# A cross-attention and mixture-of-experts kernel: the first tile's splits on other engines, two orders changed at the seam, and the last slot's weights in other buffers

## The chip, the cores and the metric

The kernel runs on one core of a Trainium2 chip. A core has five engines with their own instruction streams: PE (TensorE, matmuls), ACT (ScalarE), DVE (VectorE), POOL (GpSimd) and SP (SyncE, which here only issues DMAs). They wait for each other through semaphores. The metric is the device time in microseconds of one execution, from launch to end; lower is better.

## What is computed

x and the context are (4, 512, 512) in fp32, so there are 2048 rows. The reference, cut to what matters:

```
x = x + gamma * xattn(q=layernorm(x), k=ctx, v=ctx)      # 8 heads of 64 rows each
n = layernorm(x).reshape(2048, 512)
shared = (silu(n @ sw_gate) * (n @ sw_up)) @ sw_down      # width 1408
probs  = softmax(n @ router_w.T); top 2 of 8 experts, their weights normalised
routed = sum over the two experts of w * (silu(n @ w_gate[e]) * (n @ w_up[e])) @ w_down[e]   # width 352
out = x + routed + sigmoid(n @ shared_gate_w) * shared
```

## The kernel before

To keep fp32 accuracy on PE's fast path, each operand is split in two: a "hi" part rounded to fp32r by a copy, and a "lo" part, operand minus hi. A product is then three matmuls (hi by hi, hi by lo, lo by hi). Most work of ACT, DVE and POOL is making such pairs.

**Attention, 16 tiles of 128 rows.** Every engine runs its own hand-written `step(i)` for i from -4 on, so the order of work is what the code of each engine says. For tile t, DVE takes statistics of xb (`first_norm`, `aggregate`, `variance`), POOL makes the inverse deviation (`inverse_deviation`), the shift (`shift`) and the normed queries xn (`queries`), then the pairs kh, kl of the keys cn and qh, ql of the queries (`keys_hi`, `queries_hi`, `queries_lo`, `keys_lo`, lines 527 to 546). PE's `scores(t, par, c)` (L1249) waits for ql and kl before its first chunk. DVE takes the maximum of the scores, ACT the exponential.

**Shared layer, 4 blocks of 512 rows by 11 chunks of 128 columns** (`block2`), with the routing worked out beside it on DVE. POOL scatters row numbers and weights into a table in DRAM, which SP had filled with the padding row at the start (`meta_d`, written by 8-byte pieces from `meta`), and loads back before the routed layer.

**Routed layer, 39 slots of 128 gathered rows** (`over_slots`; slot s is of one expert, numbered 0 to 38). For slot s PE runs: transposes of the rows of s+2 (`rows3`), gate matmuls of s+1, transposes of the hidden rows of s (`hidden_T`), up matmuls of s+1, then `down3(s)`, three groups of three 512-wide matmuls. The third group needs the last 96 rows of the down weights, which POOL splits (`down_tail`, L666 the copy, L668 the subtraction); the first two groups' weights are split by ACT (`down_hi`) and DVE (`down_lo`). There is one buffer each for gate, up and down weights (wg3, wu3, wd3): the down weights of slot s can be written only when `down3(s-1)` is over (semaphore e_d3). ACT weighs the result into y3 (`weigh`), and POOL scatters it with an accumulating DMA into `out` (`scatter`, L658). A scatter waits until the one before has landed, since two slots may hold the same row:

```
if s == 0: ...
else:
    g.wait_ge(st_y[(s + 1) % 2], 16 * ((s + 1) // 2))
g.wait_ge(a_y, s + 1)
```

POOL's order in a slot is `gather(s+4)`, `down_tail(s+1)`, `scatter(s)`.

## Time and profile before

| | us |
|---|---|
| median of 3 runs | 883.13 |
| the three runs | 881.38, 883.13, 884.84 |
| the profiled execution, its own time | 884.11 |
| the profiled execution, from first to last instruction | 882.3 |
| PE busy | 851.3 (96%) |
| DVE, ACT, POOL busy | 565.9, 502.3, 451.4 |
| mean granted PE clock, as a share of full | 0.990 |

The profile is of one execution. The span is the time between its first and last instruction, and the 1.8 us beside it lie outside of any instruction. Busy PE time is the sum of its matmuls, and the remaining 31 us are waits at the start, in between and at the end. All times below are us from the start of the span.

### The profile page before, as it was taken

The numbers are of one execution on the slowest core, as the hardware profiler recorded it, in microseconds if no ns is written. First come the engines' busy times: TensorE is split into PE (matmuls) and PEld (weight loads), VectorE is DVE, ScalarE is ACT, GpSimd is POOL, SyncE is SP. The second block draws the span as 40 slices with busy tenths as digits, with TensorE's granted clock in tenths as the row PEclk, the third lists the DMA queues.
The fourth block names the chain that finished last, engine by engine and source line by source line (L and its number), as shares of the span: only waits on it lengthen the run. The fifth ranks groups of instructions, "written<-read, shape, count | busy, mean of one in ns | idle before, by whom it ended". The sixth has DMA issues, their size and how long they took to land.

```text
span 882.3 us, 13764 instructions
## 1 busy us (share of the span) xinstructions
PE 851.3 (96%) x4624; PEld 710.1 (80%) x4624; DVE 565.9 (64%) x817; ACT 502.3 (57%) x860; POOL 451.4 (51%) x434
## 2 busy tenths in 40 slices
PE   4999999999999999999999999999999999999993
PEld 3677777777788888888888888888999999999992
DVE  4899999999656414321212121117999999999991
ACT  3899999999754211211112111115888888888881
POOL 6567888876700000153330000002899999999983
PEclk9999999999999999999999999999999999999996
DMA  9214443321353212000320023547643444443442
GB/s 113 68 63 132 132 150 100 121 83 73 132 167 108 81 50 96 1 0 16 130 22 6 0 96 103 192 156 272 200 93 72 82 86 71 77 89 72 74 70 36
DMA packets 63237, 81.24 MB, mean 92 GB/s; under 512 B 15370, under 2 KB 34826, under 8 KB 63187
## 3 DMA queue, kind: packets, MB, share of 16 engines
q1 hardware_dynamic: 53426, 60.14, 22.1%
q0 software_dynamic: 9760, 20.49, 13.0%
q8 instruction: 25, 0.41, 0.2%
q14 instruction: 26, 0.20, 0.1%
HBM read 53.01 MB, written 27.60 MB: 91 GB/s over the span
## 4 chain that ended last, share of the span: by engine, by line
PE 94%; POOL 2%; DVE 1%; issue 1%; ACT 1%; DMA 0%; POOLq 0%; DVEq 0%; ACTq 0%
PE scores L1390 9%; PE scores L1388 9%; PE scores L1389 9%; PE scores L1249 7%; PE bank L1258 6%; PE bank L1402 5%; PE bank L1404 5%; PE bank L1403 5%; PE bank L1272 4%; PE bank L1496 3%; PE bank L1497 3%; PE bank L1495 3%; PE bank L1274 3%; PE scores L1471 3%; PE scores L1473 3%; PE scores L1472 3%
## 5 line engine op out<-in xcount | busy, mean ns | idle before, releaser
L1041 DVE TENSOR_TENSOR sg<-scores,sg 128x512 f32<-128x512 f32 x44 | 30.4, 692 | 200.9 <-PE scores L1390 200.8
L1388 PE MATMUL scores<-x_hl,wsp 128*128 128x512 f32 x352 | 137.2, 390 | 0.0
L1390 PE MATMUL scores<-x_hl,wsp 128*128 128x512 f32 x352 | 137.0, 389 | 0.0
L1389 PE MATMUL scores<-x_hl,wsp 128*128 128x512 f32 x352 | 136.9, 389 | 0.0
L632 POOL DMA_INDIRECT slot_rows<-msrc,posi x32 | 35.0, 1094 | 171.3 <-PE scores L1390 164.9
L647 POOL DMA_INDIRECT xg<-x_normed_rows,meta x39 | 40.3, 1034 | 160.5 <-PE scores L1412 141.9
L789 ACT ACTIVATE sg<-scores 128x512 f32<-128x512 f32 x44 | 26.3, 598 | 158.5 <-PE scores L1390 158.5
L701 ACT ACTIVATE pb<-scores,negmax 128x512 f32<-128x512 f32 x128 | 88.1, 694 | 12.8 <-DVE negmax L953 12.8
L796 ACT ACTIVATE hh<-sg 128x512 fp32r<-128x512 f32 x44 | 27.8, 631 | 114.7 <-DVE sg L1041 100.0
L963 DVE TENSOR_TENSOR ptl<-bank,pth 128x512 fp32r<-128x512 f32 x128 | 87.1, 682 | 8.4 <-ACT pth L707 8.0
L707 ACT ACTIVATE pth<-bank 128x512 fp32r<-128x512 f32 x128 | 76.7, 600 | 12.2 <-PE bank L1258 11.1
L953 DVE TENSOR_REDUCE negmax<-scores 128x2 f32<-128x1024 f32 x64 | 77.5, 1212 | 6.0 <-PE scores L1249 6.0
L668 POOL TENSOR_TENSOR wd<-wex,wd 96x512 fp32r<-96x512 f32 x39 | 79.7, 2043 | 3.3
L1258 PEld LDWEIGHTS bank<-ident,pb 128*128 128x128 f32 x512 | 61.2, 142 | 23.9 <-issue 9.8
L1258 PE MATMUL bank<-ident,pb 128*128 128x128 f32 x512 | 79.7, 280 | 0.2 <-DVE ptl L963 0.2
L1390 PEld LDWEIGHTS scores<-x_hl,wsp 128*128 128x128 f32 x352 | 66.1, 188 | 13.8
L1389 PEld LDWEIGHTS scores<-x_hl,wsp 128*128 128x128 f32 x352 | 66.1, 188 | 13.7
L1388 PEld LDWEIGHTS scores<-x_hl,wsp 128*128 128x128 f32 x352 | 66.1, 188 | 13.5
L1157 DVE TENSOR_TENSOR wg<-wex,wg 128x1408 fp32r<-128x1408 f32 x39 | 64.0, 1642 | 12.4 <-ACT wg L842 12.4
L658 POOL DMA_INDIRECT out<-y,meta x39 | 64.9, 1664 | 12.9 <-issue 5.8
L1402 PE MATMUL bank<-wsp,hh 128*128 128x512 f32 x176 | 68.8, 391 | 0.8 <-DVE tot_s L1111 0.6
L1404 PE MATMUL bank<-wsp,hl 128*128 128x512 f32 x176 | 68.5, 389 | 0.0
(177 smaller groups left out, 2231.2 us busy)
## 6 DMA issues: line engine op xcount, KB each, us to landing
wex<-in_L_ffn_w_gate SPq DMA_DIRECT2D x8, 704.0 KB, 4.5
wex<-in_L_ffn_w_up SPq DMA_DIRECT2D x8, 704.0 KB, 6.3
xb<-in_x SPq DMA_DIRECT2D x16, 256.0 KB, 2.8
cn<-in_ctx SPq DMA_DIRECT2D x16, 256.0 KB, 2.9
x_rows<-xb SPq DMA_DIRECT2D x16, 256.0 KB, 2.1
x_normed_rows<-x2n SPq DMA_DIRECT2D x16, 256.0 KB, 2.0
x_normed_transposed<-x2T SPq DMA_DIRECT2D x16, 256.0 KB, 2.0
x_hl<-x_normed_transposed SPq DMA_DIRECT2D x4, 1024.0 KB, 5.4
```

The source lines that it names most:

```text
L658: g.indirect_dma_start(out=out, out_offset=bass.IndirectOffsetOnAxis(ap=meta[:, s, 0:1], axis=0), in_=y3[s % 2][:, :], in_offset=None, com ...
L668: gp.tensor_tensor(wd3[0:IR, 1, c], wex[0:IR, e, 2 * W3 + (IC - 1) * H:EW], wd3[0:IR, 0, c].bitcast(F32), ALU.subtract).then_inc(g_wd, 1)
L701: sc.activation(pb[t % 2][s][:, c, :], bSS[c % 2][:, s, :], ACT.Exp, bias=negmax[:, c, s:s + 1], scale=1.0, accum_out=rsum[:, c, s:s + 1]) ...
L707: sc.activation(pth[n % 4][:, :], bT[P_BANK[n]][:, :], ACT.Copy).then_inc(a_pth, 1)
L953: ve.tensor_reduce(negmax[:, c, :], bSS[c % 2][:, :, :], AX_X, ALU.max, negate=True).then_inc(d_max, 1)
L963: ve.tensor_tensor(ptl[n % 4][:, :], bT[P_BANK[n]][:, :], pth[n % 4][:, :].bitcast(F32), ALU.subtract).then_inc(d_ptl, 1)
L1258: ins = te.transpose(bT[P_BANK[n]][:, q * P:(q + 1) * P], pb[par][s][:, q, c * P:(c + 1) * P], ident[:, :])
L1388: te.matmul(bk[:, :], hi, xhi, start=(h == 0), stop=False)
L1389: te.matmul(bk[:, :], hi, xlo, start=False, stop=False)
L1390: ins = te.matmul(bk[:, :], lo, xhi, start=False, stop=(h == HC - 1))
L1402: te.matmul(bY[tt][:, :], th, hi, start=(c == 0), stop=False)
L1404: ins = te.matmul(bY[tt][:, :], tl, hi, start=False, stop=(c == SC - 1))
```

## The change

There are five edits.

1. *First tile.* The keys' pair of tile 0 is made on DVE (`first_keys`), the queries' hi part on ACT (`first_queries_hi`), the lo part on DVE after the statistics of tile 1 (`first_queries_lo`). POOL makes xn of tile 0 only, and its pairs from tile 1 on. PE's first scores wait for qh and the keys' pair, and only their third term for ql.
2. *SP's queue at the start.* The gamma and router loads come ahead of the third tile of x; the two stores of padding rows go to step 2; the fill of the table in DRAM goes behind the first `load_rows` in the shared layer.
3. *Seam.* On ACT and DVE the gate weights of slot 1 are split ahead of the activation and product of slot 0.
4. *Last slot.* Its down weights are written into wg3 and wu3, which are free once the gate and up matmuls of the last slot are over. On PE the hidden transposes of slot 38 move into `down3(37)`, between its second and third group. ACT weighs slot 37 after the hi part of slot 38's hidden rows.
5. *Scatter 36.* POOL issues it ahead of `down_tail(37)`.

The diff, cut to its core (the declarations of two semaphores, the new empty lines and the unchanged bodies are left out):

```diff
@@ SP @@
+            def pads():
                 sp.wait_ge(g_zero, 1)
                 sp.dma_start(out[T:T + P, :], zrow[:, :]).then_inc(st_pad, 16)
                 sp.dma_start(xn_d[T:T + P, :], zrow[:, :]).then_inc(st_pad, 16)
+            def empty_slots():
                 sp.wait_ge(g_const, N_CONST)
                 sp.dma_start(meta_d.rearrange("(s p) c -> p s c", p=P), meta[:, :, :]).then_inc(st_meta0, 16)
...
+                if i == 2:
+                    pads()
...
             load_values(1)
+            small_ones()
             load_x(2)
-            small_ones()
...
             load_rows(0)
+            empty_slots()
             load_block(2, 0)
@@ POOL @@
                 g.wait_ge(g_nmr[0], t + 1)
+                after(g, ql_done, 1 if t == 1 else 0)
                 gp.tensor_scalar(xn[:, :], ...
...
+                after(g, kl_done, 1 if t == 1 else 0)
...
                 if there(i + 1):
                     queries(i + 1)
+                if there(i + 1) and i + 1 > 0:
                     keys_hi(i + 1)
                     queries_hi(i + 1)
...
-                if there(i + 1):
+                if there(i + 1) and i + 1 > 0:
                     queries_lo(i + 1)
                     keys_lo(i + 1)
...
             def down_tail(s, e):
-                after(g, e_d3, s)
+                if s < SLOTS - 1:
+                    after(g, e_d3, s)
...
+                w, c = wd3, slice((IC - 1) * H, IC * H)
+                if s == SLOTS - 1:
+                    g.wait_ge(e_u3, SLOTS)
+                    w, c = wu3, slice(0, H)
...
+                    if s == SLOTS - 3:
+                        scatter(s)
                     if s + 1 < SLOTS:
                         down_tail(s + 1, experts[j])
-                    scatter(s)
+                    if s != SLOTS - 3:
+                        scatter(s)
@@ ACT @@
+            def first_queries_hi():
+                act.wait_ge(g_xn, 1)
+                sc.activation(qh[0][:, :], xn[:, :], ACT.Copy).then_inc(a_q0, 1)
...
+            def last_down_hi(e):
+                act.wait_ge(e_g3, SLOTS)
+                sc.activation(wg3[:, 0, 0:2 * H], wex[:, e, 2 * W3:2 * W3 + 2 * H], ACT.Copy).then_inc(a_wd, 1)
...
+            gate_hi(1, e1)
             silu3(0, 0)
-            gate_hi(1, e1)
             up_hi(1, e1)
...
-                if not last_slots(s, 1):
+                if not last_slots(s, 2):
                     down_hi(s + 1, e1)
-                weigh(s, 2 * i + j // 2, j)
+                elif not last_slots(s, 1):
+                    last_down_hi(e1)
+                if isinstance(s, int) and s == SLOTS - 1:
+                    weigh(s - 1, 2 * i + (j - 1) // 2, j - 1)
+                if not (isinstance(s, int) and s == SLOTS - 2):
+                    weigh(s, 2 * i + j // 2, j)
@@ DVE @@
+            def first_keys():
+                dve.wait_ge(ld_cn[0], 16)
+                ve.tensor_copy(kh[0][:, :], cn[0][:, :]).then_inc(d_k0, 1)
+                dve.wait_ge(d_k0, 1)
+                ve.tensor_tensor(kl[0][:, :], cn[0][:, :], kh[0][:, :].bitcast(F32), ALU.subtract).then_inc(kl_done, 1)
+            def first_queries_lo():
+                dve.wait_ge(a_q0, 1)
+                ve.tensor_tensor(ql[0][:, :], xn[:, :], qh[0][:, :].bitcast(F32), ALU.subtract).then_inc(ql_done, 1)
...
+                if i == -1:
+                    first_keys()
                 if there(i + 2):
                     first_norm(i + 2)
+                if i == -1:
+                    first_queries_lo()
...
+            gate_lo(1, e1)
             hidden3(0, 0)
-            gate_lo(1, e1)
...
+                elif not last_slots(s, 1):
+                    last_down_lo(e1)
@@ PE @@
-                    pe.wait_ge(ql_done, t + 1)
+                    if isinstance(t, int) and t == 0:
+                        pe.wait_ge(a_q0, 1)
+                    else:
+                        pe.wait_ge(ql_done, t + 1)
...
+                    if isinstance(t, int) and t == 0 and c == 0 and n == 2:
+                        pe.wait_ge(ql_done, 1)
...
             def down3(s, j):
+                w, tail = wd3, (wd3, (IC - 1) * H)
+                if isinstance(s, int) and s == SLOTS - 1:
+                    w, tail = wg3, (wu3, 0)
...
                     if c == IC - 1:
                         pe.wait_ge(g_wd, s + 1)
+                        w, at = tail
+                        if isinstance(s, int) and s == SLOTS - 2:
+                            hidden_T(s + 1, j + 1)
...
-                hidden_T(s, j)
+                if not (isinstance(s, int) and s == SLOTS - 1):
+                    hidden_T(s, j)
```

The order of the instructions at three places, of the kernel before and then of the changed one. First POOL at the end, from the down weights of slot 37 to the last scatter (wd and wu are the weight buffers, wex the experts' weights, y the weighed rows; "waits" names semaphores):

```order
L666 ISA [waits e_d3]
L666 COPY wd_147<-wex 96x512
L668 TENSOR_TENSOR wd_147<-wex,wd_147 96x512 [waits g_wh]
L658 DMA out<-y_148,meta 2176x512 [waits a_y,st_y1]
L666 ISA [waits e_d3]
L666 COPY wd_147<-wex 96x512
L668 TENSOR_TENSOR wd_147<-wex,wd_147 96x512 [waits g_wh]
L658 DMA out<-y_149,meta 2176x512 [waits a_y,st_y0]
L658 DMA out<-y_148,meta 2176x512 [waits a_y,st_y1]
```

```order
L670 DMA out<-y_148,meta 2176x512 [waits a_y,st_y1]
L683 ISA [waits e_d3]
L683 COPY wd_147<-wex 96x512
L685 TENSOR_TENSOR wd_147<-wex,wd_147 96x512 [waits g_wh]
L683 ISA [waits e_u3]
L683 COPY wu_143<-wex 96x512
L685 TENSOR_TENSOR wu_143<-wex,wu_143 96x512 [waits g_wh]
L670 DMA out<-y_149,meta 2176x512 [waits a_y,st_y0]
L670 DMA out<-y_148,meta 2176x512 [waits a_y,st_y1]
```

The first scatter shown, of slot 36, moved up by three rows, past both instructions of slot 37's down weights. The second pair of weight rows, of slot 38, now writes wu and waits for the up matmuls instead of `down3(37)`.

Second, PE in the last two slots, from the second group of `down3(37)` to the first matmul of `down3(38)` (hT are the transposed hidden rows, h the hidden rows):

```order
L1495 MATMUL bank<-wd_147,hT_150 128x512
L1496 MATMUL bank<-wd_147,hT_150 128x512
L1497 MATMUL bank<-wd_147,hT_150 128x512
L1495 MATMUL bank<-wd_147,hT_150 128x512 [waits g_wd]
L1496 MATMUL bank<-wd_147,hT_150 128x512
L1497 MATMUL bank<-wd_147,hT_150 128x512
L1482 MATMUL scores<-ident,h_144 128x128 [waits d_ht,d_h]
L1482 MATMUL scores<-ident,h_144 128x128 x2
L1495 MATMUL bank<-wd_147,hT_146 128x512 [waits a_y,d_wd,d_ht]
```

```order
L1564 MATMUL bank<-wd_147,hT_150 128x512
L1565 MATMUL bank<-wd_147,hT_150 128x512
L1566 MATMUL bank<-wd_147,hT_150 128x512
L1544 MATMUL scores<-ident,h_144 128x128 [waits d_ht,d_h,g_wd]
L1544 MATMUL scores<-ident,h_144 128x128 x2
L1564 MATMUL bank<-wd_147,hT_150 128x512
L1565 MATMUL bank<-wd_147,hT_150 128x512
L1566 MATMUL bank<-wd_147,hT_150 128x512
L1564 MATMUL bank<-wg_142,hT_146 128x512 [waits a_y,d_wd,d_ht]
```

The transposes of slot 38 moved ahead of the third group of `down3(37)`, and the wait for g_wd, POOL's part of the weights, moved from that group to the transposes in front of it.

Third, DVE at the seam, behind the outputs of the shared layer (xT are the transposed rows of slot 1):

```order
L1206 MEMSET h_145 128x32
L1177 TENSOR_TENSOR xT_141<-scores,xT_141 128x512 [waits a_xt]
L1183 TENSOR_TENSOR h_144<-scores,h_144 128x352 [waits e_u3,a_sl]
L1157 ISA [waits a_wg]
L1157 TENSOR_TENSOR wg_142<-wex,wg_142 128x1408
L1192 ISA [waits a_wu]
L1192 TENSOR_TENSOR wu_143<-wex,wu_143 128x1408
L1197 TENSOR_TENSOR wd_147<-wex,wd_147 128x1024 [waits a_wd]
```

```order
L1261 MEMSET h_145 128x32
L1227 TENSOR_TENSOR xT_141<-scores,xT_141 128x512 [waits a_xt]
L1207 ISA [waits a_wg]
L1207 TENSOR_TENSOR wg_142<-wex,wg_142 128x1408
L1233 TENSOR_TENSOR h_144<-scores,h_144 128x352 [waits e_u3,a_sl]
L1242 ISA [waits a_wu]
L1242 TENSOR_TENSOR wu_143<-wex,wu_143 128x1408
L1252 TENSOR_TENSOR wd_147<-wex,wd_147 128x1024 [waits a_wd]
```

The subtraction of slot 1's gate weights moved ahead of the product h of slot 0.

## Rows read from the trace of the kernel before

**Rows 1.** The chain that ended last, by engine, on the page.

```profile
PE 94%; POOL 2%; DVE 1%; issue 1%; ACT 1%; DMA 0%; POOLq 0%; DVEq 0%; ACTq 0%
```

**Rows 2.** PE's waits in the span: total us, times, longest.

```profile
PE scores L1249 <- POOL kl L546: 10.4, 1, 10.4
PE bank L1495 <- DVE hT L1187: 3.5, 1, 3.5
PE bank L1471 <- DVE wg L1157: 1.7, 1, 1.7
```

**Rows 3.** The chain in order of time, first tile: start us, us, what.

```profile
5.75 0.77 POOL xn L525
6.51 0.56 POOL kh L542
7.08 0.57 POOL qh L531
...
7.72 1.26 POOL ql L536
8.99 1.23 POOL kl L546
...
10.35 2.93 PE scores L1249 x12
```

**Rows 4.** The page's costliest groups: busy us, mean ns of one, idle before.

```profile
L796 ACT ACTIVATE hh<-sg 128x512 fp32r<-128x512 f32 x44 | 27.8, 631 | 114.7 <-DVE sg L1041 100.0
L963 DVE TENSOR_TENSOR ptl<-bank,pth 128x512 fp32r<-128x512 f32 x128 | 87.1, 682 | 8.4 <-ACT pth L707 8.0
```

**Rows 5.** Timeline to 14 us: start us, us, engine, line, idle before and releaser.

```profile
7.02 0.69 DVE L926 BATCH_NORM_STATS2 stats<-xb 128x6 f32<-128x512 f32 x1 [2.48 <-DMA xb<-in_x]
...
11.35 0.66 PE L1249 MATMUL scores<-kh,ql 64*128 64x512 f32 x2
```

**Rows 6.** Timeline from 13 us, the same kind of matmul pair.

```profile
27.37 0.39 PE L1249 MATMUL scores<-kh,ql 64*128 64x512 f32 x2
```

**Rows 7.** Timeline at the seam.

```profile
604.51 1.37 ACT L842 ACTIVATE wg<-wex 128x1408 fp32r x1
...
605.24 0.65 DVE L1177 TENSOR_TENSOR xT<-scores,xT 128x512 fp32r<-128x512 f32 x1
...
606.57 1.61 DVE L1157 TENSOR_TENSOR wg<-wex,wg 128x1408 fp32r<-128x1408 f32 x1
...
608.33 0.40 PE L1471 MATMUL bank<-wg,xT 128*128 128x352 f32 x1 [1.66 <-DVE wg L1157]
```

**Rows 8.** Window at the seam: stretch, us, PE busy, granted clock, DMA, GB/s.

```profile
608.00:613.00 5.00, 4.67 (x20) 0.66 1.06 391
```

**Rows 9.** Timeline of slot 36, POOL and ACT.

```profile
855.39 1.59 POOL L658 DMA_INDIRECT out<-y,meta  x1 [0.17 <-issue]
...
858.71 0.67 ACT L882 ACTIVATE y<-bank,meta 128x512 f32<-128x512 f32 x1
```

**Rows 10.** Timeline of the last two slots.

```profile
862.13 1.57 POOL L658 DMA_INDIRECT out<-y,meta  x1 [0.16 <-issue]
...
863.03 0.40 PE L1495 MATMUL bank<-wd,hT 96*128 96x512 f32 x1
...
863.26 0.40 PE L1496 MATMUL bank<-wd,hT 96*128 96x512 f32 x1
...
867.00 1.63 POOL L658 DMA_INDIRECT out<-y,meta  x1 [0.90 <-DMA out<-y,meta]
...
871.35 0.69 ACT L882 ACTIVATE y<-bank,meta 128x512 f32<-128x512 f32 x1 [5.32 <-PE bank L1497]
872.80 1.55 POOL L658 DMA_INDIRECT out<-y,meta  x1 [4.17 <-ACT y L882]
```

**Rows 11.** POOL's copy of down weights: ns min/median/max.

```profile
L666 POOL CAST wd<-wex x39: 602/1357/1947, 603.4 to 864.2; 96x512 fp32r x38, 96x512 fp32r<-96x512 f32 x1
```

**Rows 12.** POOL's subtraction for down weights: ns min/median/max.

```profile
L668 POOL TENSOR_TENSOR wd<-wex,wd x39: 1257/2153/2163, 604.1 to 864.8; 96x512 fp32r<-96x512 f32 x39
```

21 lines of the change are left out of this document (14 added, 7 removed).

## Prediction

> **What bounds the kernel now.** I read the page first, then PE's waits, then the chain of work at the start, then the timelines around PE's three long waits. The chain that ended last is 94% PE [rows 1], so a change pays where PE stands still or where the chain isn't PE's. PE's waits name three places and little else: 10.4 us at the start for POOL's kl, 1.7 us for slot 1's gate weights, and 3.5 us at the end [rows 2]. The change touches all three. In between nothing changes that PE waits for, so what is won at the start should be carried to the end.
>
> **The start.** In the chain POOL makes xn from 5.75 to 6.52, then kh, qh, ql and kl one after the other (0.56 + 0.57 + 1.26 + 1.23 us), and PE starts at 10.35 [rows 3]. After the change three engines share this. The hi part of the queries is one ACT copy of 128x512; the nearest row is 0.63 us [rows 4]. With the 0.13 us that lie between kl's end (10.22) and PE's start [rows 3] as the price of the hand-over to PE, and half of that for the one to ACT, PE could start at 6.52 + 0.07 + 0.63 + 0.13 = 7.35, so 3.0 us earlier. The keys' pair is two DVE instructions of at most some 0.68 us each [rows 4] (the copy has no row on DVE, and I take the subtraction's), begun right after tile 0's statistics, and is done before the hi queries. The lo queries stand behind tile 1's statistics on DVE: these start when x arrives at 7.02 and take 0.69 [rows 5], and 0.68 for the subtraction make 8.4. PE wants ql with its third term, which began 1.00 us after the first (10.35 to 11.35) [rows 3, 5], so at 8.35: it waits for nothing or 0.1.
>
> DVE and POOL now work at once on SBUF. What that may cost is seen on POOL's down weights: the copy takes 0.60 at its shortest and 1.36 in the median, the subtraction 1.26 and 2.15 [rows 11, 12], and the long ones are those that DVE works beside. POOL's small instructions and xn now run beside DVE's new pair, which POOL made before. I bound the start's gain by 3.0 (no mutual slowing) and 3.0 - 2 x 0.68 = 1.6 (POOL's chain waits out both DVE instructions). I take 2.6, nearer to the free end, because DVE starts its pair while POOL is still before its 0.77 us instruction.
>
> The Trainium skill, SBUF — State Buffer, "Who interferes with whom", speaks against this edit: it says that a DVE instruction in a two-port mode, or with two SBUF inputs, and a GpSimd one exclude each other for the whole instruction, the later one being blocked. The rows of POOL's lengthened copies agree as to the sign. By that rule the start would give 1.6 instead of 2.6.
>
> POOL loses four instructions for tile 0, 3.6 us, so tile 1's pairs, which the new order starts later on DVE's side, aren't late for PE. The two padding stores and the fill of the table cost nothing at their new places: nobody waits for them before the routing, and PE, which is what ends there, doesn't depend on SP's queue at that place. If that cover were gone, it would be the time of one load at most, under 1 us.
>
> **The seam.** DVE ends the rows' split at 605.24 + 0.65 = 605.89, waits for slot 0's up matmuls, makes the product, and starts the gate subtraction at 606.57. ACT's copy of the same weights ended at 604.51 + 1.37 = 605.88, and comes earlier after the change. So the subtraction can start at 605.95, 0.6 us earlier, and PE's wait of 1.66 becomes 1.0 [rows 7]. The product, 0.5 us on DVE, comes behind it and is wanted by PE only after the gate matmuls. Behind PE's wait there is a second loss: over the 5 us from 608 the granted clock is 0.66 of full [rows 8], which is full and half of it in turn, 2.4 and 1.2 GHz, although PE is busy. Half rate for (1 - 0.66) x 5 = 1.7 us of work lost. With a wait of 1.0 us I think the clock more likely stays up, since waits of that kind and shorter elsewhere went without a fall (the mean over the whole execution is 0.99). So the seam gives 0.6 + 1.7 = 2.3, or 0.6.
>
> **The end.** This term is small although PE's 3.5 us wait is removed, since another chain takes over. Scatters must land one after the other: scatter 37 was released at 867.00 by the landing of scatter 36, issued at 862.13, so one costs 4.87 from issue to issue. The last one went at 872.80, after y at 871.35 + 0.69 [rows 10]. After the change:
> - Scatter 36 needs y of slot 36, ready at 858.71 + 0.67 = 859.4, and the landing of scatter 35, 855.39 + 4.87 = 860.26 [rows 9, 10]. It starts at 860.26 and holds POOL for 1.6, to 861.85.
> - Only then comes POOL's part of slot 37's down weights. I take 1.36 for the copy and 1.7 for the subtraction, between its 1.26 and 2.15, as DVE ends on the way [rows 11, 12]: done at 864.9. PE wants them at 863.03 [rows 10], and now has the transposes of slot 38 behind the same wait. PE stands still for 1.9 us in front of slot 38's transposes. This is the wait that takes the place of the one removed.
> - Slot 38's part follows at once, with DVE idle: 0.60 + 1.26 [rows 11, 12], done at 866.8. Scatter 37 goes at 867.05 with the 0.16 of issue. Its y is ready in time: 864.9, 0.25 for transposes, three matmuls at 0.23 [rows 10], then 0.2 + 0.67, is 866.7.
> - The last scatter waits for the landing: 867.05 + 4.87 = 871.9, against 872.80: a gain of 0.9. PE, some 2.5 us behind its stall for nine more matmuls and the hidden rows, has y of slot 38 ready by about 870, so it no longer sets the end.
> I take 0.8. With the shortest POOL durations for both pairs scatter 37 could go at 865.8, a gain of 2.1; with the longest for the first pair (1.95 and 2.15) at 868.1, a loss of 0.2. Edit 5 by itself is worth about nothing: without it scatter 37 would go at 867.0 too, by the landing of scatter 36, and PE's wait would not arise.
>
> **The sum.** 2.6 + 0.6 + 1.7 + 0.8 = 5.7 off the profiled execution's 884.11, which is 878.4. That execution is 0.98 over the median, and the other runs need not have lost the clock at the seam: counting 0.7 of the 1.7 as usual in them, 883.13 - 4.7 is 878.4 as well.
>
> **Rivals.**
> - *The clock falls at the seam as before.* For it: a wait of 1.66 was enough, and 1.0 isn't far. Against: less than two thirds of that wait are left. 884.11 - 4.0 = 880.1.
> - *POOL and DVE block each other at the start*, as in the skill's rule. Then the start gives 1.6: 884.11 - 4.7 = 879.4. For it: the doubled durations of POOL's copy. Against: its small instructions hold the port briefly.
> - *The end gives 2.1 or more*, POOL's four instructions being short: 884.11 - 7.0 = 877.1. For it: they are short where DVE is idle. Against: DVE splits slot 38's weights just then.
> - *The end loses*: POOL's chain is longer than worked out, scatter 37 late by 1 us or more, and PE's 1.9 us wait halves the clock, which delays y of slot 37. The tail term turns to -0.5: 879.7 to 881.
> - *The start is swallowed.* Matmuls of the same kind last 0.66 us in the first tile [rows 5] and 0.39 at 27.37 [rows 6]: PE runs at its lower rate until some time before 27, and nothing in these rows says what lets it rise. If it rises at the same absolute time as before, some of the 2.6 is lost: 881.
> - *Slower.* The same mechanism, worse: PE's earlier start is broken up by waits, and the rate rises much later than before. Each us of lateness costs half a us. To undo 5.7 it must be 11 us late, and to make the kernel slower by 0.5% 20 us. At 22 us late: 884.11 - 5.7 + 11 = 889.4. Against it: the new order adds no wait of PE in these tiles that I can find, and it had risen by 27 us with the old one.
>
> **Chances and range.** About 0.5% (4.4 us, so 878.7) is what a measurement of this kernel can tell from no change. The forecast has 0.55, of which some two thirds lies under 878.7; the clock at the seam 0.18; the port 0.08; a better end 0.08; a worse end 0.05; the swallowed start 0.03; slower 0.03. That gives faster 0.53, same 0.44, slower 0.03. The forecast's own range is 876.8 to 879.8. The whole range reaches from 875.8, a better end with the whole start, to 880.9, the clock and the worse end.
>
> **What would show it.** In the profile after: PE's first matmul near 7.5 instead of 10.35; PE's wait for the gate weights near 1.0, with the clock in the 5 us behind it at 1.0 or again near 0.66; no wait of PE for the last down weights, but one of about 2 us for POOL's subtraction of slot 37, in front of the transposes; the last scatter released by a DMA, not by ACT. I am wrong if PE's first matmul is later than 8.5, if PE still waits over 1.5 at the seam, if scatter 38 is released by ACT, or if new waits arise in the attention tiles.

## The result and the profile after

The changed kernel takes 877.43 us in the median of 9 runs (876.32 to 879.82), the kernel before 883.13 in 9 runs taken with them (880.50 to 885.06). The ratio is 0.9949, 95% interval 0.9935 to 0.9962. The forecast was 878.4, with a range of 875.8 to 880.9.

PE's waits after: total us, times, longest.

```profile
PE scores L1311 <- ACT qh L754: 7.3, 1, 7.3
PE scores L1544 <- POOL wd L685: 1.9, 1, 1.9
PE scores L1474 <- DMA xg<-x_normed_rows,meta: 1.3, 1, 1.3
...
PE bank L1533 <- DVE wg L1207: 1.1, 1, 1.1
...
PE bank L1564 <- DVE hT L1237: 0.5, 1, 0.5
```

Against [rows 2], the wait at the start is 3.1 us shorter and has changed its releaser from POOL's kl to ACT's qh, the one at the seam went from 1.7 to 1.1, and the 3.5 us at the end became 1.9 + 0.5. The third row is new: a gather of rows for the routed layer comes late. Nothing in the forecast names it.

The start in the timeline (start us, us, engine, line, idle before and releaser):

```profile
4.34 0.42 DVE L1014 CAST kh<-cn 128x512 fp32r<-128x512 f32 x1
4.58 0.61 POOL L524 TENSOR_TENSOR rstd<-vare,mhalf 128x1 f32<-128x1 f32 x1 [1.33 <-DVE vare L979]
4.79 0.69 DVE L1016 TENSOR_TENSOR kl<-cn,kh 128x512 fp32r<-128x512 f32 x1
5.30 0.32 POOL L528 TENSOR_SCALAR nmr<-aggr,rstd 128x1 f32<-128x1 f32 x1
5.72 0.77 POOL L535 TENSOR_SCALAR xn<-xb,rstd,nmr 128x512 f32<-128x512 f32 x1
...
6.52 0.63 ACT L754 ACTIVATE qh<-xn 128x512 fp32r<-128x512 f32 x1 [4.45 <-POOL xn L535]
7.18 0.69 DVE L1020 TENSOR_TENSOR ql<-xn,qh 128x512 fp32r<-128x512 f32 x1 [0.71 <-ACT qh L754]
...
7.25 0.80 PE L1311 MATMUL scores<-kh,qh 64*128 64x512 f32 x2 [7.25 <-ACT qh L754]
```

POOL ends xn where it did before [rows 3], ACT copies for 0.63, and PE starts 0.10 after it. DVE's keys pair (4.34 to 5.48) runs beside POOL's first two instructions and is over when xn starts.

The seam, and the new wait behind it. The row at 611.50 is slot 1's part of the down weights, the one at 615.49 the last load of expert 7, and the one at 617.76 slot 5's gather:

```profile
603.00 1.62 DVE L1207 TENSOR_TENSOR wg<-wex,wg 128x1408 fp32r<-128x1408 f32 x1
...
604.77 0.40 PE L1533 MATMUL bank<-wg,xT 128*128 128x352 f32 x1 [1.08 <-DVE wg L1207]
...
611.50 1.92 POOL L683 CAST wd<-wex 96x512 fp32r x1 [6.03 <-PE bank L1566]
...
615.49 0.80 SPq L472 DMA_DIRECT2D wex<-in_L_ffn_w_down  x1
...
617.76 0.99 POOL L659 DMA_INDIRECT xg<-x_normed_rows,meta  x1 [0.31 <-issue]
...
625.90 0.66 PE L1474 MATMUL scores<-ident,xg 128*128 128x128 f32 x4 [1.29 <-DMA xg<-x_normed_rows,meta]
```

The window behind the seam, its columns stretch, us, the busy time of PE, its weight loads, DVE, ACT and POOL, granted clock, DMA, GB/s. The granted clock is 1.00, where [rows 8] has 0.66:

```profile
605.00:610.00 5.00, 5.00 (x32) 4.81 (x32) 4.53 (x6) 2.86 (x5) 0.48 (x1) 1.00 1.04 367
```

The end, from the weighing of slot 36 to the last scatter:

```profile
854.48 0.67 ACT L913 ACTIVATE y<-bank,meta 128x512 f32<-128x512 f32 x1
...
856.41 1.56 POOL L670 DMA_INDIRECT out<-y,meta  x1 [3.66 <-DMA out<-y,meta]
857.39 1.20 POOL L683 CAST wd<-wex 96x512 fp32r x1
...
858.68 2.12 POOL L685 TENSOR_TENSOR wd<-wex,wd 96x512 fp32r<-96x512 f32 x1
...
860.86 0.55 PE L1544 MATMUL scores<-ident,h 128*128 128x128 f32 x3 [1.91 <-POOL wd L685]
...
862.15 0.69 ACT L913 ACTIVATE y<-bank,meta 128x512 f32<-128x512 f32 x1 [0.21 <-PE bank L1566]
...
863.60 1.57 POOL L670 DMA_INDIRECT out<-y,meta  x1 [0.89 <-ACT y L913]
866.39 0.69 ACT L913 ACTIVATE y<-bank,meta 128x512 f32<-128x512 f32 x1 [3.55 <-PE bank L1566]
868.51 1.55 POOL L670 DMA_INDIRECT out<-y,meta  x1 [3.34 <-DMA out<-y,meta]
```

The last scatter now waits for a landing and not for y, as forecast. But from y of slot 36 to the last scatter it takes 868.51 - 854.48 = 14.03, against 872.80 - 858.71 = 14.09 before [rows 9, 10]: the end gave 0.06.

**Where the time went.** The same event in both profiles, and how much earlier it is after:

| event | before | after | earlier | step |
|---|---|---|---|---|
| PE's first matmul | 10.35 | 7.25 | 3.10 | start 3.10 |
| slot 1's first gate matmul | 608.33 | 604.77 | 3.56 | less 0.12, wait 0.58 |
| transposes of slot 3's rows | 616.25 | 611.09 | 5.16 | clock 1.60 |
| transposes of slot 5's rows | 629.82 | 625.90 | 3.92 | gather -1.29, 0.05 other; net of the clock 0.36 |
| y of slot 36 | 858.71 | 854.48 | 4.23 | 0.31 over 230 us |
| the last scatter | 872.80 | 868.51 | 4.29 | end 0.06 |

The two profiled executions took 884.11 and 879.82, 4.29 apart. The medians are 5.70 apart, since the profiled run of after is the longest of its nine. In its profile PE's rate rises late (last section), which may be what makes it long.

### The profile page after: what moved, and what is told of

The parts are those of the page before. It is cut to its first block, busy times and chain, and to the rows that moved or that the text cites. A ratio compares the mean times of both kernels' runs of the same rounds, so it can differ in the third digit from the quotient of the medians.

```text
span 878.1 us, 13766 instructions
## 1 busy us (share of the span) xinstructions
PE 849.9 (97%) x4624; PEld 708.6 (81%) x4624; DVE 566.7 (65%) x820; ACT 503.4 (57%) x861; POOL 447.3 (51%) x430
## 4 chain that ended last, share of the span: by engine, by line
PE 92%; POOL 2%; issue 1%; DMA 1%; DVE 1%; ACT 1%; POOLq 0%; ACTq 0%; DVEq 0%
PE scores L1450 9%; PE scores L1451 9%; PE scores L1452 9%; PE scores L1311 7%; PE bank L1320 6%; PE bank L1464 5%; PE bank L1465 5%; PE bank L1466 5%; PE bank L1334 4%; PE bank L1336 3%; PE bank L1564 3%; PE bank L1565 3%; PE bank L1566 3%; PE bank L1533 3%; PE bank L1535 3%; PE bank L1534 3%
## 5 line engine op out<-in xcount | busy, mean ns | idle before, releaser
L659 POOL DMA_INDIRECT xg<-x_normed_rows,meta x39 | 38.5, 988 | 160.0 <-PE scores L1474 141.6
L670 POOL DMA_INDIRECT out<-y,meta x39 | 64.8, 1662 | 16.1 <-DMA out<-y,meta 9.5
```

The costliest lines, as they stand in the source:

```text
L670: g.indirect_dma_start(out=out, out_offset=bass.IndirectOffsetOnAxis(ap=meta[:, s, 0:1], axis=0), in_=y3[s % 2][:, :], in_offset=None, com ...
```

## The experiments

Ratios are to the kernel before, run in the same batch; its medians were 882.71, 882.66 and 882.76 in the three batches. A difference between two experiments of less than some 1 us in their medians isn't told apart.

**1. Edit 5 undone.** Scatter 36 goes behind slot 37's down weights again.

```diff
-                    if s == SLOTS - 3:
-                        scatter(s)
                     if s + 1 < SLOTS:
                         down_tail(s + 1, experts[j])
-                    if s != SLOTS - 3:
-                        scatter(s)
+                    scatter(s)
```

> The changed kernel with edit 5 undone: GpSimd makes its part of slot 37's down weights first and issues scatter 36 behind it. Theory (the chain of scatters and GpSimd's order set the end): in the changed kernel slot 37's part is done 1.9 us after PE wants it, and scatter 37 goes at 863.6 of 878.1. Undone, PE's 1.9 us wait is gone, scatter 36 goes some 1.5 us later (about 857.9), scatter 37 at its landing (4.9 later, about 862.9), the last one at 867.8 instead of 868.5: 0.7 us faster. Rival A (PE's wait sets the end): 1.9 us faster. Rival B (issuing scatter 36 early is what gives the end its gain): 0.5 us or more slower.

Measured: 877.54, ratio 0.9938 (0.9925 to 0.9951). The timeline at the end:

```profile
854.32 0.67 ACT L910 ACTIVATE y<-bank,meta 128x512 f32<-128x512 f32 x1
855.42 2.15 POOL L685 TENSOR_TENSOR wd<-wex,wd 96x512 fp32r<-96x512 f32 x1
857.73 1.57 POOL L670 DMA_INDIRECT out<-y,meta  x1 [0.16 <-issue]
...
862.73 1.57 POOL L670 DMA_INDIRECT out<-y,meta  x1 [1.43 <-DMA out<-y,meta]
867.68 1.55 POOL L670 DMA_INDIRECT out<-y,meta  x1 [3.38 <-DMA out<-y,meta]
```

POOL's subtraction ends at 857.57, before PE wants it, and PE's 1.9 us wait is gone. Counted from y, scatter 36 goes 1.5 later than in the changed kernel (3.41 and 1.93), but 37 is released by a landing and not by y, and from y of slot 36 to the last scatter it takes 13.36 instead of 14.03. So edit 5 costs 0.7 in the profile. The medians (877.54 and 877.43) don't show so little.

**2. Edit 3 undone.** On ACT and DVE the activation and the product go ahead of slot 1's gate weights again.

```diff
-            gate_hi(1, e1)
             silu3(0, 0)
+            gate_hi(1, e1)
...
-            gate_lo(1, e1)
             hidden3(0, 0)
+            gate_lo(1, e1)
```

> The changed kernel with edit 3 undone: the gate weights of slot 1 behind the activation and product of slot 0. Theory (a PE wait of 1.66 us lets the clock fall, one of 1.1 us does not, and what the seam gains beyond 1.3 us is given back because the rows of slot 4 aren't there earlier): PE's wait for slot 1's gate weights is 1.6 to 1.7 again, the clock over the 5 us behind it 0.66, that costs 2.1 us; PE's 1.29 us wait for the gathered rows of slot 4 goes to nothing. Net 0.8 us slower. Rival A (the clock stays up also with 1.66, the fall before was chance): 0.5 us later at the seam, the rows' wait shrinks by as much, net 0. Rival B (no give-back): 2.1 us slower.

Measured: 879.71, ratio 0.9969 (0.9957 to 0.9982). PE's wait at the seam, and the window there:

```profile
PE bank L1533 <- DVE wg L1207: 1.7, 1, 1.7
```

```profile
605.00:610.00 5.00, 5.00 (x31) 4.56 (x30) 4.09 (x6) 3.94 (x5) 0.58 (x1) 1.00 1.04 365
```

The 1.66 us wait is back (PE goes on at 602.69), and behind it the granted clock stayed at 1.00. So the longer wait doesn't by itself bring the clock down. From the first gate matmul of slot 1 to the transposes of slot 5's rows it takes 624.23 - 602.69 = 21.54 us here, with the clock up, and 629.82 - 608.33 = 21.49 in the kernel before, with the clock down: the late gather eats what the clock saves. The six runs fall in two, 877.95 to 878.91 at a mean clock of 0.994, and 880.51 to 880.61 at 0.988 or 0.992; in which stretch these three lost the clock isn't recorded. None of the three expectations came: the theory had the clock fall and the gather's wait go, rival A had the clock right but expected no loss, and the median is 2.2 above that of experiment 1.

**3. Expert 7's loads held for a gather.** The new wait looked like a gather that shares the DMA engines with the last expert's weights. This holds them for the gather of slot 4.

```diff
                 if e == E - 3:
                     store_out(NB - 1)
+                if e == E - 1:
+                    sp.wait_ge(ld_xg[0], 16 * 3)
                 load_expert(e)
```

> The changed kernel, and SP holds the loads of expert 7's weights until the gathered rows of slot 4 have landed. Theory (the gather of slot 4 takes 8 us because it shares the 16 DMA engines with the last experts' loads, which are issued up to that time): the gather lands within 5 us, PE's 1.29 us wait is gone, 1.3 us faster. Rival A (the gather is slow by itself or by GpSimd's side): the wait stays, 0. Rival B (the held load is late for slot 7): a new wait of ScalarE for expert 7 near 640 us, and a gain under 1.3 or a loss.

Measured: 878.42, ratio 0.995 (0.9937 to 0.9963). The wait remained, at 1.39 us. The experiment missed: slot 4's gather landed just as the loads came up and held them for only 0.3 us, so they went at 608.46, ahead of slot 5's gather. It says nothing of the cause.

**4. Edits 1 and 2 alone**, on the kernel before. The part on SP, cut to its core, beside edit 1 as in the diff of the change:

```diff
+                if i == 2:
+                    pads()
...
+            small_ones()
             load_x(2)
-            small_ones()
...
             load_rows(0)
+            empty_slots()
```

> The kernel before with edits 1 and 2 alone: the first tile's splits on ScalarE and VectorE and SP's queue reordered; seam and end as before. Theory (what is won at the start is carried to the end): PE's first matmul at 7.25 instead of 10.35, all later times 3.1 us earlier, the last scatter at 869.7, 3.1 us faster (ratio 0.9965). Rival (it is swallowed on the way, by a later rise of PE's rate or by the experts' loads): the first matmul at 7.25 but the last scatter less than 2 us earlier.

Measured: 878.50, ratio 0.9958 (0.9944 to 0.9971), 4.2 us in the median. PE starts at 7.50 and waits as before at the end (3.5 us) and at the seam (1.66). There the granted clock stayed at 1.00, and the late gather makes PE wait 1.60. The gain is carried to the end, as the theory had it, and is larger than its 3.1: in the profile the last scatter goes at 867.19, 5.6 us earlier than before, of which some 2.6 is an earlier rise of PE's rate in the first tiles (last section).

**5. Expert 7's loads held for slot 5's gather.** As 3, on the right semaphore.

```diff
+                if e == E - 1:
+                    sp.wait_ge(ld_xg[1], 16 * 3)
                 load_expert(e)
```

> The changed kernel, and SP holds expert 7's loads until the gathered rows of slot 5 have landed. The run before held them for the rows of slot 4, which land before expert 7's loads come up, so it held nothing; the rows that PE waits for are those of slot 5. Theory (they are late because they share the DMA engines with expert 7's loads): the gather lands in 5 us or less instead of 8.1, PE's wait of 1.3 to 1.7 us is gone, 1.3 us faster within one mode of the start. Rival A (slow by itself): the wait stays. Rival B: ScalarE or PE now waits for expert 7 near 640 us.

Measured: 877.13, ratio 0.995 (0.9931 to 0.9968). The timeline has slot 5's gather, the four loads and slot 6's gather, and then PE's transposes of slot 6's rows:

```profile
614.81 0.98 POOL L661 DMA_INDIRECT xg<-x_normed_rows,meta  x1 [0.31 <-issue]
619.47 0.37 SPq L466 DMA_DIRECT2D wex<-in_L_ffn_w_gate  x1
...
620.98 0.73 SPq L472 DMA_DIRECT2D wex<-in_L_ffn_w_down  x1
621.50 0.98 POOL L661 DMA_INDIRECT xg<-x_normed_rows,meta  x1 [0.31 <-issue]
...
630.33 0.66 PE L1476 MATMUL scores<-ident,xg 128*128 128x128 f32 x4 [1.98 <-DMA xg<-x_normed_rows,meta]
```

Slot 5's gather lands in 4.7 us (the loads start then), against 8.1 in the changed kernel, and its wait is gone. Slot 6's gather now goes just behind the four loads, takes 8.8 us and makes PE wait 1.98. The cause is shown: a gather that is in flight with an expert's 2.1 MB takes about twice its usual 4.2 us. Holding the loads moved the wait by a slot.

**6. Edit 4 alone**, on the kernel before (the last slot's down weights in wg3 and wu3). Two places of POOL and PE; the rest, on ACT and DVE too, is as in the diff of the change:

```diff
+                if s == SLOTS - 1:
+                    g.wait_ge(e_u3, SLOTS)
+                    w, c = wu3, slice(0, H)
...
-                hidden_T(s, j)
+                if not (isinstance(s, int) and s == SLOTS - 1):
+                    hidden_T(s, j)
```

> The kernel before with edit 4 alone: the last slot's down weights in other buffers, its transposes moved, no other edit. Theory (the chain of scatters sets the end): PE's wait at the end falls from 3.5 to under 1 us, but the last scatter is released by the landing of scatter 37 and goes only 0.7 to 0.9 us earlier than 872.8 less what the start and the seam differ by: from y of slot 36 to the last scatter 13.3 us instead of 14.1. Rival (PE's chain sets the end): 3 us or more faster, the last scatter released by ScalarE.

Measured: 881.80, ratio 0.9996 (0.9984 to 1.0009), so within what can't be told from nothing. In the profile the clock stayed up at the seam, behind a wait of 1.67 that this kernel didn't touch, and PE waits 1.4 us for slot 5's gather. The last scatter goes 13.24 us behind y of slot 36 (857.22 to 870.46), against 14.09 before: 0.85 gained. It agrees with 1: edit 4 is worth the 0.8, and edit 5 takes it back.

**7. Slot 37's last rows on ACT and DVE.** POOL drops its copy and subtraction for slot 37, so scatter 36 can go first and PE needn't wait for POOL.

```diff
@@ POOL @@
-                    if s + 1 < SLOTS:
+                    if s + 1 < SLOTS and s + 1 != SLOTS - 2:
                         down_tail(s + 1, experts[j])
@@ ACT @@
+                if isinstance(s, int) and s == SLOTS - 2:
+                    sc.activation(wd3[0:IR, 0, (IC - 1) * H:IC * H], wex[0:IR, kept["e"], at:EW], ACT.Copy).then_inc(a_t37, 1)
@@ DVE @@
+                    dve.wait_ge(a_t37, 1)
+                    ve.tensor_tensor(wd3[0:IR, 1, (IC - 1) * H:IC * H], wex[0:IR, kept["e"], at:EW],
+                                     wd3[0:IR, 0, (IC - 1) * H:IC * H].bitcast(F32), ALU.subtract).then_inc(d_t37, 1)
@@ PE @@
-                        pe.wait_ge(g_wd, s + 1)
+                        if isinstance(s, int) and s >= SLOTS - 2:
+                            pe.wait_ge(*((d_t37, 1) if s == SLOTS - 2 else (g_wd, s)))
+                        else:
+                            pe.wait_ge(g_wd, s + 1)
```

> The changed kernel, and the last 96 rows of slot 37's down weights are split by ScalarE and VectorE instead of GpSimd. Theory (GpSimd's work between scatters 36 and 37 costs the end): scatter 36 goes as early as in the changed kernel, PE's 1.9 us wait for GpSimd is gone, scatter 37 goes at the landing of 36, 5 us behind it, and the last one 5 us behind that: from y of slot 36 to the last scatter 12 us instead of 14.0, 2.0 us faster. Rival A (landings are slower when they follow each other at once): under 1 us. Rival B (ScalarE's and VectorE's added work delays PE in slot 37): a new wait of PE and under 1 us.

Measured: 876.37, ratio 0.9928 (0.9913 to 0.9943). The timeline at the end:

```profile
853.41 0.67 ACT L914 ACTIVATE y<-bank,meta 128x512 f32<-128x512 f32 x1
855.11 1.55 POOL L671 DMA_INDIRECT out<-y,meta  x1 [3.43 <-DMA out<-y,meta]
...
860.40 1.57 POOL L671 DMA_INDIRECT out<-y,meta  x1 [0.83 <-DMA out<-y,meta]
865.28 1.55 POOL L671 DMA_INDIRECT out<-y,meta  x1 [3.32 <-DMA out<-y,meta]
```

Now y of slot 36 to the last scatter takes 11.87: 2.2 less than in the changed kernel. All three scatters are released by landings, with 5.3 and 4.9 between them, so the chain of scatters alone sets the end.

**8. PE busy from the start.** 20 matmuls of ones, whose result nobody reads, on PE ahead of everything.

```diff
+            pe.wait_ge(g_const, 4)
+            for n in range(20):
+                te.matmul(bT[2][:, 0:P], ones[:, :], ones[:, :], start=True, stop=True)
```

> The changed kernel with 20 matmuls of a constant tile, whose result nobody reads, on PE ahead of the first scores, in the time in which PE only waits. Theory (which of two modes a run falls into is set by when PE's rate rises in the first tiles, at about 12 us or at about 22 us, and earlier work of PE brings it forward): the rate is full at the latest at the third chunk of scores in every run, the run times lie together, and the median is at least 1 us below that of the changed kernel. Rival (the rise comes at a time that PE's earlier work doesn't move, or the modes come from elsewhere, as the DMAs): both modes stay, no gain; if the 20 matmuls outlast the wait, a loss.

Measured: 876.94, ratio 0.9938 (0.9922 to 0.9953). The timeline at the start (the row counts 40 for the 20), and a later window:

```profile
1.37 6.77 PE L1365 MATMUL bank<-ones 128*128 128x128 f32 x40 [1.37 <-POOL mhalf L503]
8.07 0.50 PE L1311 MATMUL scores<-kh,qh 64*128 64x512 f32 x2
8.40 0.40 PE L1311 MATMUL scores<-kl,qh 64*128 64x512 f32 x2
```

```profile
16.00:19.00 3.00, 3.00 (x14) 2.12 (x12) 1.51 (x4) 2.02 (x5) 0.79 (x2) 0.50 0.00 0
```

The first pairs of scores take 0.40 us instead of the 0.66 of [rows 5], the full rate. But they start 0.8 later, PE soon waits for its partners (2.02 us busy of the 4 from 12 on), and from 16 to 19 the granted clock is 0.50. The matmul that the changed kernel's profile has at 37.20 comes at 35.47, 1.7 us earlier, but in the profiles with the early rise (last section) it comes at 34.27 to 34.63 without any extra matmuls. The gain of 1 us in the median didn't come: 876.94 isn't told apart from the changed kernel's 877.43.

**9. Edit 1 alone**, with SP's old order: as 4, without the part on SP. The diff is against experiment 4:

```diff
-                if i == 2:
-                    pads()
...
-            small_ones()
             load_x(2)
+            small_ones()
...
             load_rows(0)
-            empty_slots()
```

> The kernel before with edit 1 alone: the first tile's splits on ScalarE and VectorE, SP's queue in its old order. Theory (the new order of SP's queue only moves the landing of tile 1's x, which nothing waits for on the path to PE's first matmul): the first matmul between 7.2 and 7.6 as with both edits; the lo queries, behind tile 1's statistics, at 7.7 instead of 7.2, which costs PE's third term at most 0.1 us. Same time as with edits 1 and 2 (median 878.5 to 879). Rival (the old order's padding stores and its table fill with 5000 small packets hold up loads that now are wanted 3 us sooner): a wait of VectorE or GpSimd for a load before 25 us, and 1 us or more slower than with both.

Measured: 881.66, ratio 0.9999 (0.9982 to 1.0015). My expectation missed by 3 us, and the rival held. PE starts at 7.54 all the same. SP's queue, and two DMA issues from the trace's DMA view (KB, us to landing), the fill of the table and, for the last section, the load that reads it back:

```profile
5.19 0.49 SPq L389 DMA_DIRECT2D slot_rows<-meta  x1
5.72 9.82 SPq L342 DMA_DIRECT2D xb<-in_x  x1
15.66 0.36 SPq L347 DMA_DIRECT2D cn<-in_ctx  x1
```

```profile
slot_rows<-meta SPq DMA_DIRECT2D x1, 39.0 KB, 19.3
meta<-slot_rows SPq DMA_DIRECT2D x1, 39.0 KB, 5.6
```

DVE's statistics of the fourth tile of x:

```profile
24.67 0.69 DVE L937 BATCH_NORM_STATS2 stats<-xb 128x6 f32<-128x512 f32 x1 [3.85 <-DMA xb<-in_x]
```

The fill of the table is 39 KB in 8-byte pieces, some 5,000 packets, and needs 19.3 us. The load of x that was issued behind it holds SP's queue for 9.8 us and lands at 5.72 + 18.92 = 24.64; POOL then waits 4.2 us for the load of cn behind that. In the kernel before the same load of x landed 15.7 us after its issue, at 21.4, and the statistics start at 24.19 without waiting for it; in the changed one they start at 21.09. With the old SP order an earlier PE runs into a load that isn't earlier. Experiments 4 and 9 move the two padding stores with the fill, so no run separates the three. The trace points to the fill: from 12 to 16 us all DMA engines together move 2 GB/s, while the load of x is in flight.

In this profile, one of the long runs of its kernel, PE's granted clock is also 0.51 from 14 to 18 and 0.64 from 18 to 22. Of the 12 runs 11 have a mean granted clock of 0.992 or less, against 3 of the 9 of experiment 4. How the 3.2 us between the medians of 9 and 4 divide between the late load and the clock isn't settled.

**10. Experiment 7, with expert 7's loads spread.** They wait for the landing of slot 5's, 6's and 7's rows in turn.

```diff
+                if e == E - 1:
+                    sp.wait_ge(ld_xg[1], 16 * 3)
                 load_expert(e)
...
+                if e == E - 1:
+                    sp.wait_ge(ld_xg[0], 16 * 4)
                 sp.dma_start(w[:, HC * I:2 * HC * I].rearrange("p (c i) -> p c i", c=HC),
...
+                if e == E - 1:
+                    sp.wait_ge(ld_xg[1], 16 * 4)
                 sp.dma_start(w[:, 2 * HC * I:2 * HC * I + (IC - 1) * H].rearrange("p (c h) -> p c h", c=IC - 1),
```

> The changed kernel, with slot 37's last 96 rows on ScalarE and VectorE as in the run before, and expert 7's four loads spread: the first behind the landing of the rows of slot 5, the second behind those of slot 6, the last two behind those of slot 7. Theory (a gather is late when two MB of an expert's load stand with it in the DMA engines, and is in time beside 0.7 MB): no wait of PE for gathered rows over 0.3 us in slots 4 to 7, 1.2 us faster than with the tail alone, median about 875. Rival (each part still delays its gather): waits of 0.5 us or more remain and the gain is under 0.5.

Measured: 876.12, ratio 0.9941 (0.9919 to 0.9964). No gather takes over 4.9 us, and PE waits for none; its transposes of rows come evenly, each 6.68 us behind the last. The theory's mechanism held, but its 1.2 us didn't show: six runs from 875.36 to 880.47 don't tell it apart from 7.

**11. Experiment 10, with 17 matmuls of ones** ahead, as in 8.

```diff
+            pe.wait_ge(g_const, 4)
+            for n in range(17):
+                te.matmul(bT[2][:, 0:P], ones[:, :], ones[:, :], start=True, stop=True)
```

> The same as e10, with 17 matmuls of a constant tile on PE ahead of the first scores (20 outlasted the wait by 0.7 us). Theory: PE's rate is full from the first scores on in the profile and no run falls into the slow mode of the start throughout; 0.5 to 1.5 us faster than e10 in the median. Rival (the waits of 1 us in the first tile let the rate fall again, as in e8 from about 16 to 19 us, so that little is won): same as e10 within 0.5.

Measured: 876.26, ratio 0.9932 (0.9914 to 0.9951). Its 873.66 is the shortest run of the study, and its median is that of 10. In that run's profile PE's rate is full from the first scores at 7.23 on, as the theory has it, but falls again as the rival has it: the granted clock is 0.53 from 15.4 to 19, behind 1.4 us with PE busy for 0.28. Nothing is gained for certain.

**12. Edit 3 alone**, on the kernel before: the reverse of the diff of 2.

```diff
-            silu3(0, 0)
             gate_hi(1, e1)
+            silu3(0, 0)
...
-            hidden3(0, 0)
             gate_lo(1, e1)
+            hidden3(0, 0)
```

> The kernel before with edit 3 alone: the gate weights of slot 1 ahead of the activation and product of slot 0. Theory: PE's wait there 1.1 instead of 1.66 us; the fall of the clock behind it, which only some runs of the kernel before have, appears in none; in runs without a fall 0.6 us are won at that place. Median 0.6 to 1 us below that of before (ratio 0.9990 to 0.9994). Rival (the fall was in most runs): 2 us faster. Second rival (given back by the wait for slot 5's rows): no change.

Measured: 881.54, ratio 0.9986 (0.9974 to 0.9999), 1.2 us in the median. PE's wait at the seam is 1.08, the clock behind it 1.00, and PE waits 1.44 us for slot 5's gather. One of its 12 runs has a mean granted clock of 0.991 or less, against 8 of the 23 of the kernel before in that batch; but experiment 6, without edit 3, has one of 12 as well, with 0.992 as the limit the shares are 4 of 12 and 9 of 23, and the mean doesn't say where in a run the clock fell. So that edit 3 makes the fall rarer isn't shown.

**The seam in eight of the profiles.** From slot 1's first gate matmul to the transposes of slot 5's rows:

| kernel | PE's wait at the seam | clock, 5 us behind it | PE's wait for slot 5's gather | us |
|---|---|---|---|---|
| before | 1.66 | 0.66 | none | 21.49 |
| 2 (seam undone) | 1.66 | 1.00 | 1.71 | 21.54 |
| 4 (start alone) | 1.66 | 1.00 | 1.60 | 21.45 |
| 6 (last slot alone) | 1.67 | 1.00 | 1.40 | 21.24 |
| 9 (edit 1 alone) | 1.66 | 1.00 | 1.66 | 21.50 |
| 12 (seam alone) | 1.08 | 1.00 | 1.44 | 21.29 |
| after | 1.08 | 1.00 | 1.29 | 21.13 |
| 10 (loads spread) | 1.08 | 1.00 | none | 19.70 |

Where the clock stays up and expert 7's loads aren't moved, slot 5's gather is late in every profile, by 0.50 (experiment 8) to 1.71 us, with any start and any end; where it fell, the gather was in time because PE came later. The fall at the seam costs 1.6 us by slot 3's rows and no more than 0.4 by slot 5's.

## Why the prediction was right, and where it wasn't

The time, the sign and all four marks that it set (PE's first matmul, the seam's wait and clock, PE's wait for slot 37's subtraction, the last scatter's releaser) came as forecast. Two terms of the sum, the clock and the end, didn't. Step by step:

- **The start, 2.6 forecast, 3.1 measured at the first matmul and 3.0 when it reaches the seam.** The free bound was the right end. POOL's small instructions took 0.61 and 0.32 us beside DVE, against 0.58 and 0.26 before: some 0.1 us of mutual slowing. Its xn took 0.77 both times, but DVE's pair was over by then, so that says nothing. The lo queries were ready at 7.87 and not 8.4, because x of tile 1 had landed by 5.78 and not at 7.02 [rows 5], and PE's third term waited for nothing. (In 9, with the old SP order, that load was there by 5.70 too, so its lateness in the kernel before wasn't the order's doing.) The Trainium skill, SBUF — State Buffer, "Who interferes with whom", has a DVE instruction with two SBUF inputs, or in a two-port mode, and a GpSimd one exclude each other. By that POOL's first instruction, begun at 4.58, could have waited until 5.48 for the end of DVE's pair, and the first matmul would come up to 0.9 us later than it did (an estimate from these rows). Here the rule's price didn't show, though DVE's subtraction at 4.79 has two inputs in SBUF and POOL worked beside it for 0.4 us.
- **"The two padding stores and the fill of the table cost nothing at their new places"** held: at their new place nobody waits for them. What failed is the step behind it, that SP's edit therefore has no share in the sum. Experiment 9 against 4 shows that it carries 3.2 of the start's 4.2 us in the median, though not how much of this is the late load and how much the clock. I had asked what the moved DMAs cost where they go, and not what they cost the load behind them where they stood. It could be seen in the trace before: the load of x behind the fill holds SP's queue for 8.92 us.
- **The seam's wait, 0.6 forecast, 0.58 measured** (1.66 to 1.08).
- **The clock at the seam, 1.7 forecast, 1.60 measured at slot 3's rows, and 0.36 at slot 5's.** The size of the loss was read rightly, and so was that the clock would stay up. What failed is the step that carries the 1.7 to the end. It is given back to slot 5's gather, which in the kernel before was hidden by the fall. Nor is the fall tied to the longer wait: it stayed away behind waits of 1.66 and 1.67 us in the profiles of 2, 4, 6 and 9. That the clock would stay up was therefore right, but the reason given, a wait under two thirds as long, isn't shown. In medians the effect of edit 3 is 1.2 (12, between 0.1 and 2.3), which agrees with the 0.6 and 0.4 of the profiles, and 2.2 (2, against 1 in the same batch), which is more; what else is in it stays open.
- **The end, 0.8 forecast, 0.06 measured.** PE's 1.9 us wait came exactly. Two links of the chain were too short. y of slot 37 was ready 8.36 us behind the start of y of slot 36, where the sum had 8.0: scatter 36 went 5.25 behind scatter 35 and not 4.87, and slot 37's subtraction took 2.12 and not 1.7. Most of these 0.8 us came back, because POOL began the copy 0.98 behind the scatter's start and not 1.6, and the copy took 1.20 and not 1.36; another 0.2 came from PE, since y started 1.35 behind the subtraction's end and not 1.14. The other link is from y's end to the scatter's issue, 0.76 us (862.84 to 863.60), where the sum had 0.35. The subtraction and this hand-over were in rows at hand: 2153 ns is the median of [rows 12], and y's end at 872.04 and the scatter at 872.80 stand in [rows 10].
- **"Edit 5 by itself is worth about nothing"**: it costs 0.7 in the profile (1, and 6 from the other side). The reason given, that scatter 37 would go at the same time without it, fails because with it y of slot 37 is late, and without it isn't.
- **Not foreseen: 1.3 us given back by slot 5's gather.** I had written that in between nothing changes that PE waits for. Counted from slot 1's first gate matmul, the gather is issued at 12.99 us after (617.76) and at 14.36 before (622.69). POOL comes to it behind its part of slot 1's down weights and scatter 0, and it starts on those when PE ends `down3(0)` (611.50 after, 616.66 before), which the full clock brought forward; SP has issued the last load of expert 7 by 11.52 (616.29) and 10.61 (618.94). So the gather goes 1.5 us behind that issue and not 3.8, overlaps more of the transfers, and takes 8.1 us instead of 7.1. Experiment 3 tells nothing of this; 5 and 10 show the cause by moving the loads. The gather's buffer is free once PE has transposed slot 3's rows, at 611.7, so it could also be issued some 6 us earlier, ahead of slot 1's down weights; no run tries this. The gather in the kernel before:

```profile
622.69 1.02 POOL L647 DMA_INDIRECT xg<-x_normed_rows,meta  x1 [0.31 <-issue]
```

The errors were of both signs: in the profile start +0.4, clock and gather -1.3, end -0.7, and +0.3 in the slots between that no step accounts for, so that 4.3 us came of the 5.7. In the medians 5.7 came, where the second form of the sum had 4.7, and there the start alone gave 4.2, more than the 3.0 of the profile. That the time came within 1 us of the forecast is in part luck. The chances don't add up as written either: two thirds of 0.55 and the better end's 0.08 make 0.45 for faster, not 0.53.

The best kernel found is that of experiment 7 (ratio 0.9928), which keeps all five edits and cures the wait that edit 5 made. Experiments 10 and 11, which add to it, aren't told apart from it.

## What to carry to other kernels

When a DMA is moved, price it at the place it leaves as well: the load behind a small transfer of thousands of pieces held the queue for 9 us, and the gain of another edit hung on the order there. When a stretch gets shorter, list what each later wait has besides the engine that became faster: the loads that ran beside it don't get earlier by as much, a gather that was just in time can be late, and a loss of clock in front of such a wait is worth less than it looks. And where one chain (here scatters that must land one by one) is within 1 us of setting the end, write out every link with its hand-over from a row, since a gain of that size is lost in two links of 0.4.

## What the runs showed of the hardware

**PE's rate in the first tiles.** In all kernels without extra matmuls PE begins at the lower rate (pairs 0.66 us long, the next one 0.43 behind), and the time at which it rises differs between executions. PE's timeline of the changed kernel, and of experiment 4, which has the same order here:

```profile
12.29 0.63 PE L1311 MATMUL scores<-kl,qh 64*128 64x512 f32 x2
...
24.20 0.39 PE L1311 MATMUL scores<-kl,qh 64*128 64x512 f32 x2
```

```profile
12.28 0.39 PE L1286 MATMUL scores<-kl,qh 64*128 64x512 f32 x2
```

The same matmuls take 0.63 in the one and 0.39 in the other. The profiles of 2, 3, 4 and 5 have the early rise, at about 12; the kernel before, the changed one and 1, 6 and 12 have it between 21 and 26, and 10 at about 20. In 7 and 9 it comes early and is lost again (0.50 from 14 to 19 in 7). The matmul that the changed kernel has at 37.20 comes 2.6 to 2.9 us earlier in the profiles with the early rise that lasts. This would explain why the profiled run of after is 2.4 over its median. All six profiles with the early rise are of kernels with the new start, and none of the three with the old start has it; if that holds over all runs, it is part of why the start is worth 4.2 in the medians and 3.0 in the profile, which no run tests. The granted clock reads 1.00 in both, from 8 to 25 us; so a record of 1.00 didn't mean the full rate before the first change of level.

Matmuls ahead of the first scores brought the full rate to them (8 and 11), and the clock fell later. In 8 it is 0.50 from 16 on, after 4 us in which PE was busy for 2.02; in 4 PE was busy for 1.87 us of the same stretch, and the clock stayed at 1.00. What decides the time of the rise or of this fall isn't shown by any run here.

**A wait of PE and its clock.** The same wait of 1.66 us was followed by 0.66 of the full clock over 5 us in one profile [rows 8] and by 1.00 in four others (2, 4, 6 and 9). The fall was nearly free all the same, since a late gather waited behind it: slot 5's rows came 21.49 us behind the seam with the fall, and 21.24 to 21.54 behind the same wait without it.

**Small pieces in a DMA.** The store of 39 KB in 8-byte pieces took 19.3 us to land in 9, 16.1 in the kernel before and 17.5 at its new place in the changed one, while 256 KB of x take 2.8 in the median. The Trainium skill, DMA: Bandwidth & Descriptors, "Bandwidth", says of loads from HBM issued on GpSimd that transfers under 64 KB are descriptor-dominated, and for this store, which SP issued, the trace agrees. But neither the size nor the number of pieces alone sets its price: the load that reads the same table back, also 39 KB in some 5,000 packets, landed in 5.6 us. What no run here separates is how much of the 18.9 us of the load behind it was the queue and how much the shared DMA engines.
